# The last unit of a gated long-convolution layer and its way into the feed-forward part: order of the VectorE and GpSimd work changed, second tile transposed on TensorE

## What is computed

```
xp = (X @ Wp + bp), cut into 4 parts of 256 channels
f  = (pos @ Wf + bf), cut into 3 filters of 2048 x 256 (pos: sines and cosines)
y  = xp[0];  for i in 0..2:  y = causal_conv(y, f[i]) * xp[i+1]     (along the rows, per channel)
x1 = layernorm(X + y)
z  = (silu(x1 @ Wg.T) * (x1 @ Wu.T)) @ Wd.T      (Wg, Wu 768 x 256, Wd 256 x 768, int32 / 127)
out = layernorm(x1 + z)
```

## Time and profile before

| | us |
|---|---|
| median of three executions | 760.33 (760.05 to 760.33) |
| profiled execution, its own time | 762.3 |
| span in that profile | 760.5 |
| mean granted TensorE clock | 0.995 of full |

### The profile page before, as it was taken

One profiled execution on the slowest core, in us unless ns is written; L12 is line 12 of the kernel. 1 busy time (PEld: TensorE's weight loads), 2 busy tenths in 40 slices (PEclk: granted clock), 3 DMA queues, 4 the chain that ended last, 5 costly groups with the idle time before them and its releaser, 6 DMA issues.

```text
span 760.5 us, 16073 instructions
## 1 busy us (share of the span) xinstructions
PE 730.5 (96%) x5936; PEld 547.8 (72%) x5936; DVE 554.1 (73%) x1083; ACT 488.0 (64%) x962; POOL 421.8 (55%) x483
## 2 busy tenths in 40 slices
PE   6999999999899999999999999789999999999995
PEld 5878878888788888888888888545665556655663
DVE  4797778777688888888888888665656666565644
ACT  3445553444378888788887665446776776777753
POOL 3445554445243444344434444789788878888653
PEclk9999999999999999999999999999999999999998
DMA  8659768999898999989999996622445335452412
GB/s 290 212 179 333 248 213 282 316 320 305 297 259 256 260 259 246 257 254 263 254 248 265 310 258 218 225 56 56 103 93 114 109 84 112 85 137 57 63 54 79
DMA packets 193676, 152.69 MB, mean 201 GB/s; under 512 B 35776, under 2 KB 177216, under 8 KB 193344
## 3 DMA queue, kind: packets, MB, share of 16 engines
q1 hardware_dynamic: 191744, 146.36, 66.5%
q10 hardware_dynamic: 1856, 5.31, 2.2%
HBM read 109.45 MB, written 34.34 MB: 189 GB/s over the span
## 4 chain that ended last, share of the span: by engine, by line
PE 86%; DVE 5%; DMA 4%; issue 2%; ACT 2%; POOL 1%; SPq 0%; DVEq 0%; POOLq 0%; ACTq 0%
PE bank L472 21%; PE bank L398 20%; PE bank L452 18%; PE bank L493 10%; PE bank L411 7%; PE bank L432 3%; PE bank L433 3%; PE bank L434 3%; DMA toep<-filter_rows 1%; DVE prod L830 1%; DMA wi<-in_WDT 1%; DMA gates<-toep 1%; DMA xt<-in_XT 1%; DVE yl L864 1%; PE bank L509 1%
## 5 line engine op out<-in xcount | busy, mean ns | idle before, releaser
L1025 POOL TENSOR_TENSOR y<-y,gate 128x512 f32<-128x512 f32 (+1 forms) x108 | 124.7, 1160 | 172.3 <-DVE y L855 160.1
L398 PE MATMUL bank<-wps,xs 128*128 128x512 f32 x768 | 183.3, 398 | 7.9 <-DVE wps L788 6.5
L452 PE MATMUL bank<-prod,ei 128*128 128x256 f32 x720 | 186.8, 382 | 0.0
L398 PEld LDWEIGHTS bank<-wps,xs 128*128 128x128 f32 x768 | 144.7, 190 | 40.5 <-POOL xs L1052 8.1
L830 DVE TENSOR_TENSOR prod<-bank,wfx 128x512 f32<-128x512 f32 x180 | 124.2, 690 | 43.5 <-PE bank L411 43.5
L1052 POOL TENSOR_TENSOR xs<-xt,xs 128x256 fp32r<-128x256 f32 x128 | 93.7, 743 | 101.4 <-ACT xs L605 101.3
L472 PE MATMUL bank<-xh,wq 128*128 128x512 f16 x384 | 145.6, 379 | 0.2
L472 PE MATMUL bank<-xl,wq 128*128 128x512 f16 x384 | 145.5, 379 | 0.0
L1044 POOL TENSOR_TENSOR hl<-hf,hh 128x512 f16<-128x512 f32 x95 | 110.7, 1168 | 53.0 <-ACT hh L669 53.0
L452 PEld LDWEIGHTS bank<-prod,ei 128*128 128x128 f32 x720 | 123.4, 191 | 11.6
L634 ACT ACTIVATE y<-bank,iscl 128x512 f32<-128x512 f32 x96 | 66.0, 687 | 90.3 <-PE bank L434 90.3
(11 more groups left out here) (81 smaller groups left out, 1220.0 us busy)
## 6 DMA issues: line engine op xcount, KB each, us to landing
toep<-filter_rows SPq DMA_DIRECT2D x43, 1024.0 KB, 7.6
gate<-gates SPq DMA_DIRECT2D x48, 512.0 KB, 4.1
xt<-in_XT SPq DMA_DIRECT2D x31, 512.0 KB, 5.5
gates<-st SPq DMA_DIRECT2D x24, 512.0 KB, 4.1
gates<-toep SPq DMA_DIRECT2D x24, 512.0 KB, 4.2
xr<-in_X SPq DMA_DIRECT2D x16, 512.0 KB, 4.6
out_x<-oo SPq DMA_DIRECT2D x15, 512.0 KB, 3.2
toep<-filter_rows SPq DMA_DIRECT2D x10, 512.0 KB, 6.3
```

What stands on the lines that cost most here:

```text
L398: mm = pe.matmul(b_proj[n % PBK][:, :], xs[:, n % XSS, hx, k, :], wps[:, hw, k, p * 512:(p + 1) * 512], start=(k == 0 and q == 0), stop=(k ...
L452: mm = pe.matmul(b_out[m % 2][:, half * W:(half + 1) * W], ei[:, h, e0 * P:(e0 + 1) * P], prod[:, n % 3, h, :], start=(h == 0), stop=(h == 1))
L1025: nc.gpsimd.tensor_tensor(y[:, u % NG, a:a + count, :], y[:, u % NG, a:a + count, :], gate[:, a:a + count, :], ALU.mult).then_inc(gated, 1)
```

## The change

Nothing that is computed changes; the order does, and tile 1's way into the feed-forward part.

- VectorE, unit 11: `gather` in odd steps from 5 on stands behind `multiply` instead of ahead of it. The statistics of chunk 0 are taken in two pairs of sequences behind `multiply(4)` and `multiply(6)`, the aggregation behind `multiply(8)`. `low_first(0, t)` stands behind `multiply(12)` and `multiply(14)`; the statistics of chunk 1 are taken in step 15.
- GpSimd: root 1 moves from step 6, where it stood ahead of `apply(11, 2)`, to step 9, behind `apply(11, 3)` and ahead of `add(1)`, which moves there from step 7; `add(2)` moves to step 13; root 2 to behind `apply(11, 7)`.
- ScalarE: `norm1(0)` in step 9, `split_first(0)` in step 11, and casts 4 and 5 behind it. `norm1(1)` moves into tile 0, behind `high_h(0, 0)`, and the split of tile 1 behind `high_h(0, 2)`.
- TensorE: `transposes(0)` stands before `state(11)`; `transposes(1)`, 8 more, in tile 0 behind block 3. Tile 1 then has no transposing DMAs, no `split_x` and no `low_x`.

```diff
@@ -242,7 +242,7 @@
         def turns(k):
-            return 16 * ((k + 1) // 2)
+            return 16 * (k // 2)
 
@@ -348,7 +348,7 @@
                     for src, dst, ready, done in ((xhn, xh, xhn_ready, xh_in), (xln, xl, xln_ready, xl_in)):
-                        sp.wait_ge(ready, k)
+                        sp.wait_ge(ready, k - 1)
                         sp.dma_start_transpose(dst[:, k % 2].rearrange("p b t n -> p (b t) n"),
@@ -366,8 +366,6 @@
                 for k in range(3):
-                    if k == 2:
-                        turn(1)
                     sp.wait_ge(x1_ready, k + 1)
@@ -453,17 +451,19 @@
 
-                def transposes():
-                    pe.wait_ge(x1n_ready, NB)
+                def transposes(k):
+                    pe.wait_ge(x1n_ready, k * NB + NB)
+                    if k:
+                        pe.wait_ge(xl_ready, KT)
                     for t in range(KT):
                         for b in range(NB):
-                            mm = pe.transpose(b_t[t][:, b * P:(b + 1) * P], x1n[:, 0, b, t * P:(t + 1) * P], ident[:])
+                            mm = pe.transpose(b_t[t][:, b * P:(b + 1) * P], x1n[:, k, b, t * P:(t + 1) * P], ident[:])
                         mm.then_inc(tr_done, 1)
...
                 def ffn_up(k, m, wt, dst):
-                    if k == 0:
-                        pe.wait_ge(xh_ready, KT)
-                        pe.wait_ge(xl_ready, KT)
+                    if k < 2:
+                        pe.wait_ge(xh_ready, k * KT + KT)
+                        pe.wait_ge(xl_ready, k * KT + KT)
                     else:
@@ -558,10 +558,10 @@
                             norm(u + 2)
-                        if k == 10 and u == NU - 1:
+                        if k == 11 and u == NU - 1:
                             pe.wait_ge(id_in, 16)
                             pe.wait_ge(toep_out, NU * NQ)
-                            transposes()
+                            transposes(0)
                         if u < NU and k < NE and k != 1:
@@ -569,7 +569,7 @@
                         if k == 14 and u == NU - 1:
-                            pe.wait_ge(w_cast, 6)
+                            pe.wait_ge(w_cast, 4)
                             pe.wait_ge(norm_sum, NU)
@@ -584,10 +584,13 @@
                             up_part(k, m)
+                        if m == 3 and k == 0:
+                            transposes(1)
                         if m == 2:
...
                                     pe.wait_ge(z_done, NU * NPAIR)
+                                    pe.wait_ge(w_cast, 6)
                                 down(k - 1)
@@ -646,15 +649,15 @@
 
-                def split_first():
-                    act.wait_ge(tr_done, KT)
+                def split_first(k):
                     for t in range(KT):
-                        nc.scalar.activation(xh[:, 0, :, t, :], b_t[t][:, :].rearrange("p (b n) -> p b n", b=NB), ACT.Copy,
+                        act.wait_ge(tr_done, k * KT + t + 1)
+                        nc.scalar.activation(xh[:, k, :, t, :], b_t[t][:, :].rearrange("p (b n) -> p b n", b=NB), ACT.Copy,
                                              scale=XS).then_inc(xh_ready, 1)
...
                     act.wait_ge(x1n_ready, k * NB + NB)
-                    if k >= 3:
+                    if k >= 4:
                         act.wait_ge(xh_in[k % 2], turns(k - 2))
@@ -746,24 +749,27 @@
                                 nc.scalar.activation(warm[:], ones[:, 0:1], ACT.Silu)
-                            if 1 <= k <= 6:
+                            if 1 <= k <= 4:
                                 cast(k - 1)
-                            if k == 8:
+                            if k == 9:
                                 norm1(0, range(NB))
-                            if k == 10:
-                                split_first()
-                            if k == 13:
-                                norm1(1, range(NB))
-                                split_x(1)
+                            if k == 11:
+                                split_first(0)
+                                cast(4)
+                                cast(5)
                 for k in range(NA):
...
                     high_h(k, 0)
+                    if k == 0:
+                        norm1(1, range(NB))
                     silu(k, 2)
...
                     high_h(k, 2)
+                    if k == 0:
+                        split_first(1)
                     if k >= 2:
@@ -869,6 +875,9 @@
                     last.then_inc(stats, 1)
+                    row_means(slot, count)
+
+                def row_means(slot, count):
                     dve.wait_ge(stats, count)
@@ -877,20 +886,25 @@
 
+                def first_pair(h):
+                    for b in (2 * h, 2 * h + 1):
+                        last = nc.vector.bn_stats(bst[:, 0, b, :], x1[:, 0, b, :])
+                    if h:
+                        last.then_inc(stats, 1)
+
                 def stats1(k, count):
...
 
-                def low_first():
-                    for t in range(KT):
-                        dve.wait_ge(xh_ready, t + 1)
-                        nc.vector.scalar_tensor_tensor(
-                            out=xl[:, 0, :, t, :], in0=b_t[t][:, :].rearrange("p (b n) -> p b n", b=NB), scalar=XS,
-                            in1=xh[:, 0, :, t, :], op0=ALU.mult, op1=ALU.subtract).then_inc(xl_ready, 1)
+                def low_first(k, t):
+                    dve.wait_ge(xh_ready, k * KT + t + 1)
+                    nc.vector.scalar_tensor_tensor(
+                        out=xl[:, k, :, t, :], in0=b_t[t][:, :].rearrange("p (b n) -> p b n", b=NB), scalar=XS,
+                        in1=xh[:, k, :, t, :], op0=ALU.mult, op1=ALU.subtract).then_inc(xl_ready, 1)
 
                 def low_x(k):
-                    dve.wait_ge(xhn_ready, k)
-                    if k >= 3:
+                    dve.wait_ge(xhn_ready, k - 1)
+                    if k >= 4:
                         dve.wait_ge(xl_in[k % 2], turns(k - 2))
@@ -965,27 +979,41 @@
                             gather(u - 1, NPAIR - 2 + k)
-                        if k >= 5 and k % 2 and u < NU:
+                        if k >= 5 and k % 2 and u < NU - 1:
                             gather(u, (k - 5) // 2)
...
                         if u == NU - 1:
-                            if k in (5, 10):
-                                stats1(k // 5 - 1, k // 5)
-                            if k == 12:
-                                low_first()
+                            if k >= 5 and k % 2:
+                                gather(u, (k - 5) // 2)
+                            if k == 4:
+                                dve.wait_ge(x1_ready, 1)
+                                first_pair(0)
+                            if k == 6:
+                                first_pair(1)
+                            if k == 8:
+                                row_means(0, 1)
+                            if k in (12, 14):
+                                low_first(0, k // 2 - 6)
+                            if k == 15:
+                                stats1(1, 2)
                 for k in range(NA):
                     product(k, 0)
-                    if k + 1 < NA:
+                    if 1 <= k < NA - 1:
                         low_x(k + 1)
                     product(k, 1)
+                    if k == 0:
+                        dve.wait_ge(mean_ready, 2)
                     if k + 2 < NA:
...
                         sum2(k - 1)
+                    if k == 0:
+                        for t in range(KT):
+                            low_first(1, t)
                     product(k, 3)
@@ -1059,14 +1087,16 @@
                             apply(u, (k - 3) // 2)
-                        if u == NU - 1 and k in (2, 7, 12):
-                            t = k // 5
+                        if u == NU - 1 and k == 9:
+                            root(0, 1)
+                        if u == NU - 1 and k in (2, 9, 13):
+                            t = k // 6
                             if t == 2:
...
                             add(t)
-                        if u == NU - 1 and k in (6, 11):
-                            root(0, k // 5)
+                        if u == NU and k == 0:
+                            root(0, 2)
                 pool.wait_ge(gated, NU * NGATE)
```

## The result

| | changed | before | ratio (95%) |
|---|---|---|---|
| first set of runs | 766.14 | 760.05 | 1.0074 (1.0063 to 1.0086) |
| second set | 764.81 | 759.56 | 1.0067 (1.0047 to 1.0087) |

Forecast was 764.3, +4.0, with a range of 761.2 to 765.7; measured are +6.1, a little beyond the upper end, and +5.3, inside it. The profiled execution of the changed kernel took 766.14, its span is 764.3. In it unit 11 stands 0.32 us earlier on the clock than in the one shown of before (`state(5)` at 480.66 for 480.98), so stretches are compared, not times of day.

The account below looks back on a forecast made before the run. TensorE, busy 96%, bounds the kernel; only `down(0)`'s start can move. Unit 11 +0.1 (-3.85 + 0.12 + 1.2 + 2.1 + 0.36 = -0.1, by the starts +0.1), tile 0 +2.6, clock +1.3: +4.0, 764.3, range 761.2 to 765.7.

Parts of the forecast that it names:

- Late states gone, the first pair for 0.12: Unit 11: three stalls from statistics or low part on VectorE go, -3.85; the first pair of statistics costs +0.12.
- Product ahead of gather: Unit 11: five even-step readouts wait for the gather still reading their bank, 0.24 each, +1.2 in all.
- the bound of 0.35: Unit 11: upper cost per waiting readout, if its weights are not loaded ahead.
- Root 1 at 489.90: GpSimd, unit 11: root 1 starts only then, behind `apply(11, 3)` that waits for a gather, making x1n 3.3 later.
- Clock, 1.3: Behind the stop before the transposes, TensorE's clock falls to half speed, costing 1.3; chance 0.50.
- Tile 0, 17.9: From `up_part(0, 0)` at 503.2 to `down(0)` at 521.1, clock up; new transposes and waits add 2.6.
- 4.16 us against 2.07, +2.1: TensorE's stop before unit 11's transposes grows from 2.07 to 4.16 as x1n comes late, costing 2.1.
- (1): Rival: the clock stays up, +2.7, 763.0, or 763.4 with late weights of waiting readouts; chance 0.24.
- (2): Rival: faster, as tile 0's waits don't come, 758.0 to 759.5; chance 0.10.
- (3): Rival: no difference; tile 0's waits other than the transposes overlap and the clock stays up, +1.0, 761.3; chance 0.09.
- (4): Rival: worse by a further stop, such as 0.14 at five readouts and the clock's full 1.7, 765.5; chance 0.07.
- 2.07 did not, 2.27 did: TensorE stops before: 2.07 at 488.4 left the clock up, 2.27 at unit 0's start preceded a fall; supports the clock term.

Follow-up runs that it names:

- the filler: The changed kernel with 27 unused matmuls into an unused bank ahead of the transposes: 763.65, ratio 1.0045 to the kernel before.
- the mended kernel: The change's idea with all four engines' orders in unit 11 and tile 0 rewritten, `add(3)` behind `low_h(0, 2)`: 755.70, ratio 0.9935 to the kernel before.
- the execution of 757.95: A profiled execution of the kernel before, run again unchanged; that run measured 760.28, ratio 0.9995.
- the kernel with the gathers behind: The mended kernel with all six gathers of unit 11 moved behind the odd product: 757.48, ratio 0.996 to the kernel before.

## Why the prediction was right in kind and somewhat short in size

Its case, a later x1n and a fallen clock, is what happened, in four profiles out of four. Point by point, as predicted and as measured:

- Late states gone, the first pair for 0.12: `state(5)` to `state(6)` is 1.33, so 0.04.
- Product ahead of gather, 0.24 a step pair: 481.99 to 484.88 is 2.89 for 2.58, so 0.31. The readout starts 0.65 after its state, as my sum had it (0.64), but then holds TensorE 0.97 (482.64 to 483.61) where I had 0.87: nearer to the bound of 0.35, in which the weights are loaded only then.
- Root 1 at 489.90 (489.58 on this clock): 489.69. The transposes at 493.38 on this clock: 493.55. The stop of 4.16 from the last matmul's slot: 4.14 (3.98 by the row).
- Clock, 1.3: the filler prices it at 1.20. The way there was in part luck. I had the clock fall after the restart, with all of the 3.4 us at half speed on work (1.7); by the stretches above it was at half speed from about 492.96 to 496.36, 0.6 of it still in the stop, so about 1.4 of work was lost.
- `up_part(0, 0)` at 504.2 on this clock, with the clock's term: 504.38.
- Tile 0, 17.9 from there to `down(0)`: 17.83, against 15.28 before. Where I had put 0.46 of waiting for x1n it is 0.36, and 0.74 for the silu of block 5 where I had 0.85, both from the last matmul's slot; the rows' 0.20 and 0.57 count from its modelled end.
- Stretch in all, 39.98 + 4.0 = 44.0: 44.13 to 44.22.

The terms of the sum were right; what was off is the baseline from which one of them is reckoned, "4.16 us against 2.07, +2.1". In the kernel before `norm1(0)` doesn't wait for root 1 (ready at 485.62) but stands behind casts 4 and 5, and cast 4 waits for a transfer:

```profile
486.48 0.84 ACT L646 ACTIVATE wq<-wi 128x768 f16<-128x768 int32 x1 [3.29 <-DMA wi<-in_WDT]
```

So TensorE's wait for x1n varies with that transfer: 0.90, 1.50 and 1.92 in the three profiles, and I had reckoned from the longest. "Moving casts 4 and 5 out of the way gains nothing here" is true of the changed kernel, but it passed over this. In the changed kernel casts 4 and 5 stand behind `norm1(0)` and the stretch hardly varies. Against the mean of three, 39.5, the change costs 4.7, not 4.2. That covers between a third and a half of the way from 4.0 to the 5.3 and 6.1 measured. The rest, 0.6 to 1.4, stays open. In the profiles only the part ahead of unit 11 varies beside the stretch, in code that is the same: `state(3)` falls at 475.1, 477.8 and 478.4 in profiles of before and at 476.2, 477.0, 477.5 and 478.1 in those of the changed kernel. Most of that spread is there where unit 0 begins (200.7 to 202.6). These are too few to tell chance from a cause.

On the rivals: (1), the clock staying up, came in none of the four profiles. Its price was right, as the filler shows. (2) and (3) rested on tile 0's waits not coming. They came. Of the rivals (4), 765.5, is nearest in number, but neither of its parts came: the readouts cost 0.31 and not 0.24 plus 0.14, and the clock cost 1.20 and not 1.7. In tile 0's waits I had not separated two causes. In the mended kernel tile 0 takes 15.5 (496.41 to 511.96: 14.7 of gate and up parts and the transposes, no waits); with the change's orders in tile 0 it takes 1.0 more; in the changed kernel 17.83. So, by subtraction between kernels and not by a run of its own, 1.3 of the 2.3 us of waits are left for chunk 1 coming late, by its statistics in step 15 and root 2 behind `add(2)` and two applies, and 1.0 for the order within the tile.

The idea of the change was sound as far as pairs of statistics go: they do fit between the products. The second tile's transposes on TensorE cost 0.9; whether they pay isn't shown, as no run orders the engines anew and keeps that tile's DMA turns. With the same pieces in another order the kernel is 4.9 us faster than before instead of 5 to 6 slower.

## What to carry to other kernels

When a small step is moved on an in-order engine, ask what its new neighbour ahead waits for: 1.6 us of small operations behind an apply that waits for another engine's gather cost 4 us. A bound measured in one profile carries the luck of that execution's transfers; take the baseline from several. A stop of TensorE can have a second price beside its length, the fall of its clock, and filling the stop with idle matmuls tells the two apart in one run.

## What the runs showed that I had not expected

- In unit 11 a stop of 3.98 us brought the clock to half each time (4 profiles), and cost 1.2 us on top in a loop that waits for VectorE anyway; stops of 0.90 to 1.92 there (four profiles) never did. But the length alone doesn't decide. Where unit 0 begins the stop was 1.92 to 2.92 in the 13 profiles, and the clock fell behind it in 11 of them, also behind stops of 1.92 and 1.93. In the other two, the execution of 757.95 (1.92) and that of the kernel with the gathers behind (1.93), it stayed up. So my reading of "2.07 did not, 2.27 did" as a matter of length was wrong, though the case it argued for came. First a further profile of the changed kernel, then the kernel with the gathers behind, the granted clock third from the end:

```profile
200.69 0.28 PE L409 MATMUL bank<-yh,ef 128*128 128x256 f16 x1 [1.93 <-DVE prod L836]
...
203.00:207.00 4.00, 4.00 (x41) 3.31 (x40) 2.29 (x4) 1.80 (x4) 0.74 (x1) 0.79 1.02 325
```

```profile
201.71 0.28 PE L409 MATMUL bank<-yh,ef 128*128 128x256 f16 x1 [1.93 <-DVE prod L847]
...
203.00:207.00 4.00, 4.00 (x49) 3.40 (x45) 3.07 (x9) 2.56 (x4) 0.00 (x0) 1.00 1.02 306
```

- Eight float32 transposes take 0.90 us at a granted clock of 1.00 and 1.74 at 0.50: they follow the granted clock.
- A float32 readout that waited for the gather starts 0.05 behind the gather's end (482.59), but holds TensorE 0.97; two readouts in a row, with no wait, take 1.73 (501.37 to 503.10 in the kernel before), 0.87 each. The idle time in its own row, 0.15, shows only half of the 0.32 by which it starts late.
